# Convolution and FFT-mixer kernel: weights prepared one pass earlier, last bias on ScalarE, products nobody reads in the first slots, and another order of the last slots

## The reference

```python
# layer 0: depthwise convolution, 25x25 taps of which every third is kept and the middle one is 0
lat = conv(x, raw_kernel * mask, padding='SAME', feature_group_count=96)
x = lat * x + bias + x
# layer 1, part 1: tokens t = 3025 positions of each image
h = relu(bn1(ln(t) @ w1.T))                       # 96 -> 192
X = fft(h, axis=tokens, norm='ortho')             # 3025 points
xr = relu(X.real * rd - X.imag * idg + rb)        # rd, idg: diagonals of r and i
xi = relu(X.imag * rd + X.real * idg + ib)
t = t + bn2(ifft(xr + 1j * xi, norm='ortho').real @ w2.T)
# layer 1, part 2: feed-forward net whose operands are rounded to fp8 (5 bit exponent, 2 bit mantissa)
h = relu(qlinear(ln(t), W1, b1))                  # 96 -> 384
t = t + qlinear(h, W2, b2)                        # 384 -> 96
```

## Time and profile before

| | |
|---|---|
| median of three runs | 4942.9 us |
| profiled execution | 4928.84 us |
| its span | 4927.0 us |
| busy: PE, DVE, ACT, POOL | 91%, 74%, 74%, 46% of the span |
| convolution | from the start to about 868 us |
| mixer | from about 868 us to the end |

### The profile page before, as it was taken

How to read it: one execution, slowest core, us unless ns; L and a number is a source line. 1 busy time by engine, 2 the same in 40 slices (tenths; PEclk the granted TensorE clock), 3 DMA queues, 4 the chain that set the end, 5 groups by cost and what they waited for, 6 DMA issues and landing times.

```text
span 4927.0 us, 170278 instructions
## 1 busy us (share of the span) xinstructions
PE 4496.8 (91%) x64799; PEld 3663.0 (74%) x64799; DVE 3649.5 (74%) x10911; ACT 3659.7 (74%) x7819; POOL 2281.3 (46%) x2602
## 2 busy tenths in 40 slices
PE   7999997699999999999999999999999999999964
PEld 6888886477777777777777777777777777777742
DVE  5444446247888888888888888888888888888865
ACT  3444443378888888888888888888888888888843
POOL 2433542144555555555555555555545455555532
PEclk9999998599999999999999999999999999999965
DMA  6877785366666666666666666666666666666541
GB/s 177 249 250 224 238 252 173 105 170 193 179 184 182 186 181 181 184 185 180 183 187 184 189 185 188 181 178 186 184 179 186 176 184 184 182 186 187 164 96 30
DMA packets 787283, 895.64 MB, mean 182 GB/s; under 512 B 241723, under 2 KB 694776, under 8 KB 774392
## 3 DMA queue, kind: packets, MB, share of 16 engines
q1 hardware_dynamic: 786200, 884.64, 63.4%
q10 hardware_dynamic: 288, 0.11, 0.0%
HBM read 500.00 MB, written 384.61 MB: 180 GB/s over the span
## 4 chain that ended last, share of the span: by engine, by line
PE 57%; DVE 12%; ACT 8%; issue 4%; DMA 0%; DVEq 0%; POOL 0%; POOLq 0%; SPq 0%; ACTq 0%
PE ps L1138 13%; PE ps L1125 10%; ACT y L912 7%; PE ps L1157 7%; PE ps L1233 5%; PE ps L1166 4%; PE ps L1182 4%; PE ps L1222 4%; PE ps L1196 4%; PE ps L1209 3%; PE ps L1112 2%; DVE y L995 1%; DVE bn L1048 1%; DVE xn L1033 1%; DVE var L972 1%
## 5 line engine op out<-in xcount | busy, mean ns | idle before, releaser
L789 POOL TENSOR_SCALAR gv<-gv 128x400 f32<-128x400 f32 (+1 forms) x512 | 489.6, 956 | 1663.8 <-DVE xn L1033 1433.7
L1138 PE MATMUL ps<-hid,fa 121*128 121x384 f32 (+1 forms) x2048 | 805.9, 476 | 43.0 <-DVE t L1057 30.8
L554 PE MATMUL cps<-toep,xin 114*128 114x190 f32 (+2 forms) x3456 | 780.7, 340 | 67.5 <-DVE xo L519 32.1
L912 ACT ACTIVATE y<-ps 128x1089 f16<-128x1089 f32 (+1 forms) x512 | 573.2, 1120 | 311.8 <-PE ps L1222 311.8
L395 ACT ACTIVATE xo<-cps 128x180 f32<-128x180 f32 (+3 forms) x576 | 367.3, 638 | 463.2 <-PE cps L557 463.1
L1125 PE MATMUL ps<-w1t,xnt 97*121 97x192 f32 x3200 | 707.0, 332 | 2.9 <-issue 2.1
L519 DVE SCALAR_TENSOR_TENSOR xo<-cps,xo 128x180 f32<-128x180 f32 (+3 forms) x576 | 361.5, 629 | 429.6 <-ACT xo L395 429.0
L554 PEld LDWEIGHTS cps<-toep,xin 114*128 114x128 f32 x3456 | 534.2, 195 | 133.7 <-issue 43.0
L1001 DVE CAST hq<-y 128x1092 fp8e5<-128x1092 f16 (+1 forms) x512 | 537.1, 1049 | 53.4 <-DVE y L995 0.9
L866 ACT ACTIVATE hid<-ps 121x384 f32<-121x384 f32 (+1 forms) x1024 | 438.9, 429 | 169.8 <-PE ps L1125 169.7
L995 DVE TENSOR_SCALAR y<-y,b1q 128x364 f16<-128x364 f16 (+1 forms) x1536 | 477.9, 366 | 105.4 <-ACT y L912 105.4
(11 more groups left out here) (110 smaller groups left out, 9702.3 us busy)
## 6 DMA issues: line engine op xcount, KB each, us to landing
a_d<-arow SPq DMA_DIRECT2D x448, 288.0 KB, 4.5
acol<-a_d SPq DMA_DIRECT2D x384, 300.0 KB
xin<-in_items SPq DMA_DIRECT2D x96, 1008.0 KB
g_d<-mixed SPq DMA_DIRECT2D x512, 150.0 KB
tok<-x_d SPq DMA_DIRECT2D x64, 1134.4 KB
out<-o_sb SPq DMA_DIRECT2D x448, 136.1 KB
x_d<-xo SPq DMA_DIRECT2D x48, 990.0 KB, 12.2
grow<-g_d SPq DMA_DIRECT2D x128, 312.0 KB, 10.5
```

Source lines behind the costliest of these rows:

```text
L554: last = nc.tensor.matmul(ps[2 * (m % DEEP)][:, (r0 - o0) * GC:(r1 - o0) * GC], xb, toep[e % 2][0:GP, c, at * GC:(at + r1 - r0) * GC], sta ...
L789: nc.gpsimd.tensor_scalar(v, v, 0.0, None, ALU.max).then_inc(v_cut, 1)
L912: nc.scalar.activation(y16[n % 2][:, :, 0:w], ps[:, MIXP:MIXP + FM, 0:w], ACT.Copy).then_inc(y16_ready, 1)
L1138: nc.tensor.matmul(ps[0:M, ROW, 0:(s1 - s0) * H], fa[:, :], hid[part][:, 0:s1 - s0, :].rearrange("p j h -> p (j h)"), start=True, stop=Tru ...
```

## The change

It has seven parts.

1. The preparation of the weights moves from pass 1 to the second half of pass 0 (VectorE before items 18, 22, 25, 28, 30, 32 and 34, ScalarE's roots before item 20).
2. The item biases of the last pass move from VectorE to ScalarE.
3. SyncE waits for the tokens of image 0 before it issues the tables `fb` and `ib`.
4. TensorE gets products that nobody reads (`keep_busy`, identity by identity, 128x128, into bank 7): 40 ahead of the slots, 2 and 3 at two places of each slot 0 to 15, and 10 ahead of the first `columns`.
5. Behind the last inverse (slots from `DRAIN` = 528) `down` writes bank 0 and goes last in the slot on TensorE, `out_down` goes last on ScalarE, and `up` no longer waits for `z_ready` of the chunk before.
6. `gate_sum` is cut into three functions and a semaphore `b_ready` is added to its first instruction; VectorE's `larger` waits for it. The order of these instructions stays.
7. `widen_bias` is cut in two and some offsets are written in another way (`RES` as `ROWS + 1` and the like), with no instruction moved.

```diff
+DRAIN = CHUNKS + INV + 1
...
         @block.scalar
         def _(act):
+            def bias_item(t, n):
...
+                act.wait_ge(gated, t * PER + n + 1)
+                v = xo[k][e % 2][:, :, n % DIL::DIL, n // DIL]
+                nc.scalar.activation(v, v, ACT.Identity, bias=cbias[:, c:c + 1]).then_inc(biased[1], 1)
...
-                    if t == 1 and n == 2:
+                    if t == 0 and n == 20:
                         act.wait_ge(w_var, 1)
...
+                    if t == PASSES - 1 and n:
+                        bias_item(t, n - 1)
+            bias_item(PASSES - 1, PER - 1)
...
-                    if t == 1 and n == 0:
+                    if t == 0 and n == 18:
                         shift_variances()
-                    if t == 1 and n == 6:
+                    if t == 0 and n == 22:
                         invert_roots()
-                    if t == 1 and n == 14:
+                    if t == 0 and n == 25:
                         refine_roots()
...
-                    if t == PASSES - 1 and n:
-                        bias_item(t, n - 1)
-            bias_item(PASSES - 1, PER - 1)
...
+        def down_bank(n):
+
+            return DOWNP if n + DOWN < DRAIN else 0
...
                 if g == FIRST + 1:
+                    sp.wait_ge(tok_in[0], 16)
                     sp.dma_start(fb[:, :, :], p["c_fb"]).then_inc(tables_in, 16)
...
+            def gate_imag(t):
...
+                nc.scalar.activation(spectrum(t, 0), column(t, 1), ACT.Abs,
+                                     scale=idg[:, hf:hf + 1]).then_inc(b_ready, 1)
...
+            for g in range(DRAIN, LAST + 1):
+                if here(g - TURN2 - 1):
+                    out_turn2(g - TURN2 - 1)
+                if g % NS == 6 and 0 <= (g + 2) // NS < B + 5:
+                    root((g + 2) // NS)
+                if here(g - UP):
+                    out_up(g - UP)
+                if here(g - DOWN):
+                    out_down(g - DOWN)
...
                 dve.wait_ge(c_ready, t + 1)
+                dve.wait_ge(b_ready, t + 1)
                 nc.vector.tensor_tensor(sv, column(t, 0), sv, ALU.max).then_inc(m_ready, 1)
...
-                pe.wait_ge(y16_ready, n + 1)
+                if n + DOWN < DRAIN:
+                    pe.wait_ge(y16_ready, n + 1)
+                else:
+                    pe.wait_ge(v_ready, CHUNKS)
+                    pe.wait_ge(m_ready, CHUNKS)
...
-                        last = nc.tensor.matmul(ps[:, DOWNP, C * j:C * (j + 1)],
+                        last = nc.tensor.matmul(ps[:, down_bank(n), C * j:C * (j + 1)],
...
-                    pe.wait_ge(z_ready, n)
+                    pe.wait_ge(z_ready, min(n, DRAIN - DOWN))
...
+            def keep_busy(times):
+                for _ in range(times):
+                    nc.tensor.matmul(ps[:, DOWNP, 0:128], ident[:, :], ident[:, :], start=True, stop=True)
+
+            keep_busy(40)
+            for g in range(FIRST, DRAIN):
+                filling = 0 <= g < GATE + 6
+                if g == GATE:
+                    keep_busy(10)
...
+                if filling:
+                    keep_busy(2)
                 if here(g - 1):
                     rows(g - 1, 1)
                 if here(g):
                     widen(g, 0)
                 if here(g - MIX):
                     mix(g - MIX)
+                if filling:
+                    keep_busy(3)
                 if here(g):
                     rows(g, 0)
...
+            for g in range(DRAIN, LAST + 1):
+                if here(g - ROWS):
+                    inverse_rows(g - ROWS)
+                if here(g - UP):
+                    up(g - UP)
+                if here(g - TURN2):
+                    turn2(g - TURN2)
+                if here(g - DOWN):
+                    down(g - DOWN)
```

More of the change, by code:

```diff
@@ L997, in widen_bias, with cast @@
                 last.then_inc(relu_ready, 1)
+            def cast(n):
+                w = (tokens(n)[1] - tokens(n)[0]) * U
+                w += w % 2
+                y, q = y16[n % 2], hq[n % 2]
                 if n >= 2:
@@ L1071, in _ @@
                 k, c = (g + 2) // NS, g % NS
-                if here(g - RES):
-                    residual(g - RES)
+                if here(g - ROWS - 1):
+                    residual(g - ROWS - 1)
                 if c == 6 and 0 <= k < B + 5:
```

69 lines of the change are left out of this document (39 added, 30 removed).

## The result

The changed kernel takes 4830.0 us (median of 4 runs, 4823.6 to 4838.0) against 4945.2 us (median of 4, 4940.8 to 4949.2; a fourth run has moved it from 4942.9) for the kernel before: ratio 0.9768, 95% interval 0.9751 to 0.9786, so 115 us or 2.3% faster. The forecast was 4822, its range 4795 to 4858: inside the range, and 8 us slower than forecast.

A forecast was written before the change was run, and what follows sets the result against it. The prediction took TensorE to bound the long middle, and waits between engines the four stretches around it. Gains of 18.3 + 22.8 + 4.5 + 18 + 5 + 51.7 = 120.3 us from 4942.9 gave 4822 us, range 4795 to 4858.

The forecast's parts named there:

- Slots 10 to 16: Mixer slots after the fill, 40.7 us before, partly at the low clock: gain 5 us (0 to 8).
- Weights in pass 0: Convolution pass 1: parameter instructions no longer blocked by GpSimd's bias once moved to pass 0; gain 18.3 us (15 to 18.5).
- Last bias on ScalarE: Convolution pass 15: item bias no longer waits for GpSimd, ScalarE fits copy and bias; gain 22.8 us (18 to 23).
- a sign of being wrong: Convolution pass 15: the prediction would be wrong if ScalarE's bias took over 0.6 us.
- Tokens ahead of the tables: Start of the mixer: first tokens arrive sooner when loaded without the tables; gain 4.5 us (2 to 6).
- Unread products: Mixer's fill: products close TensorE's holes and raise its clock to 2.4 GHz; gain 18 us (-1 to 26).
- rival 1: Mixer's fill: clock stays at 1.2 GHz, gains of 18 and 5 us fall away, total 4846 us; chance 0.13.
- Drain: Slots 528 to 553: two chunks in the chain at once, 97.6 us instead of 149.3; gain 51.7 us (20 to 64).
- GpSimd against VectorE: Drain: GpSimd's additions now fall beside VectorE's work, only bias and cast meeting them; cost 0.25 us a slot, 6 in all.
- Rival 2: Drain: GpSimd's lock holds VectorE 1.48 us on each of 25 slots, 31 us above charge, total 4853 us; chance 0.12.
- The middle: Long stretch between fill and drain: bound by TensorE at full clock, the change moves nothing there.
- rival 4: Middle: new semaphore and doubled waits stretch each of 510 slots; at 0.3 us the kernel takes 4975 us; chance 0.02.

The follow-up runs named there:

- e1: Kernel before, with only the preparation of the weights moved from pass 1 to pass 0: 4923 us, ratio 0.9961.
- e2: Kernel before, with only the item bias of the last pass moved from VectorE to ScalarE: 4917 us, ratio 0.9946.
- e3: Kernel before, with only the drain's change (`down` last in its own bank, its copy last, `up` without the late `z_ready`): 4898 us, ratio 0.9909.
- e4: Changed kernel with all unread products taken out: 4852 us, ratio 0.9821 to the kernel before.
- e8: Changed kernel with the tables loaded together with the first tokens instead of behind them: 4839 us, ratio 0.9806 to the kernel before.
- e10: Changed kernel without the 40 products ahead of the first turn, the others kept: 4832 us, ratio 0.9782 to the kernel before.
- e7: Changed kernel with its unread products on the 8-bit 121x121 identity, same number: 4855 us, ratio 0.9840 to the kernel before.
- e9: Changed kernel without the five products a slot in slots 0 to 15, the 40 and the 10 kept: 4856 us, ratio 0.9836 to the kernel before.
- e5: Changed kernel with GpSimd's two additions in the drain covering only 2 of 96 columns, output incomplete: 4815 us, ratio 0.9758 to the kernel before.
- e11: Changed kernel with four more unread products behind `down` in every slot of the drain: 4820 us, ratio 0.9760 to the kernel before.

## Why the prediction was right, and which terms were off

The five mechanisms with a kernel of their own stood: weights (e1), bias (e2) and drain (e3) alone, products (e4) and the order of tokens and tables (e8) by taking them away. Slots 10 to 16 have no run of their own. The sum was 120.3 us against 115 measured (interval of the ratio: 106 to 123), and the terms were on the whole too high: measured one by one they add up to some 110. The terms:

*Weights in pass 0*: predicted 18.3. The profiled pair showed 15.5 at the start of pass 2 and 12.9 at that of pass 15, and I first took that for a loss; over all profiles it is 17.1 and 18.5, with single ones up to 7 us apart. Right within that.

*Last bias on ScalarE*: predicted 22.8, measured 22.9 in the pair and 22.0 to the last item in e2. I had priced the bias at 0.50 us and it takes 0.60 to 0.63, which I had named as a sign of being wrong. It did no harm, because the bias starts 0.21 us before the copy has ended (789.83 against 789.52 + 0.52), so that the pair takes 0.91 us (789.52 to 790.43). The Trainium skill (ScalarE: Activation LUTs, What ACT_TABLE_LOAD costs) gives some 93 ns for the operand and as much overlap with a neighbour. The rows agree on the operand, about 0.10 us more than the copy, and not on the overlap, which is about twice that. With one overlap of 93 ns my estimate would have been 1.00; the 0.91 of the prediction takes it off twice, once at each end of the pair, and in the rows only one end overlaps. That it met the measured 0.91 is luck.

*Tokens ahead of the tables*: predicted 4.5, measured 2.8 in the pair and 3.2 by e8. The sum divided bytes by the common rate of tokens and tables; alone the tokens were there 9.65 us after their issue, against 880.43 - 867.98 = 12.45 before, with the tables beside them.

*Unread products*: predicted 18 up to slot 10, measured 19.4, but two errors cancel. A product was priced at 0.21 us at 1.2 GHz from the pitch of three transpositions; it takes 0.22 at 2.4 GHz and twice that at 1.2. The slot became 3.90 and not 3.6 for it. Against that the clock stayed high through the whole stretch, where I had let some of it fall. The 40 ahead were costed as free and are, but they are also worth nothing (e10), and the reason for rival 1's low chance was weaker than written: e7 had the holes halved and TensorE 92% busy, and the clock stayed at 0.50. With its products rival 1 was the outcome, so that the products of the change were enough was in part luck.

*Slots 10 to 16*: predicted 5, measured 0.9 in the pair. The clock is up (0.91 against 0.68), but the pitch is now 6.75 us from `columns` to `columns` in five of six slots, where before it went from 5.05 to 8.16. TensorE waits there 5.5 us for VectorE's gating, against 2.7 before: what the clock gives goes in good part into this wait. This is the term that was furthest off for its size. The pair is also at the low end: in the six kernels without products in these slots the stretch takes 39.6 to 43.0 us (e9, e4), 41.5 in the mean, and in the seven with the 32-bit products 37.5 (e5) to 39.9, 39.4 in the mean, so some 2 us is the better figure. Why kernels with the same work there differ by up to 3 us is open.

*Drain*: predicted 51.7, measured 46.0. The step that was mis-sized is "GpSimd against VectorE", charged with 0.25 us a slot or 6 in all: e5 gives 15.9, of which up to 2 may be its clock. Its reason was too narrow as well: the prediction let only bias and cast meet GpSimd's additions, and the root chains and the norm were held too (4.1 us by e5). The rest of the sum was then 91.6 against 87.4 measured in e5, 4 us too high, so that two errors partly cancel here as well. `down` came 4.63 us apart up to slot 541 and 3.59 behind it, not 3.6 and 2.8. Rival 2, which charged 31 us more for the lock, was right in kind and came true by a third. Where the additions meet VectorE's bias, as at 4733.59, the slot pays 0.95 us; the mean over 25 slots is 0.64.

The Trainium skill (SBUF — State Buffer, Who interferes with whom) describes the lock as exclusive for the whole instruction. The rows agree where VectorE's bias goes from 0.75 to 1.70 us beside 1.57 us of additions. An estimate from the rows: if all of GpSimd's time had held VectorE, it would have cost 25 times 1.48 us, 37 us, and it took 15.9. The rest of GpSimd's time met instructions that were not held (statistics and residual) or idle time.

*The middle*: nothing moved and rival 4 is out, but it was 7.2 us longer in the pair. In the profiles of all fourteen kernels, whose middles do the same work, it took between 3612.0 (e11) and 3633.6 us (e10), and the 3614.4 of before is near the short end. The four kernels without `b_ready` take 3622.9 in the mean and the ten with it 3624.1, so the new semaphore and the doubled waits, which the prediction put at nothing, cost no more than the wander hides. That wander, with the one of the convolution, is why 107 us of stage gains in the pair, 110 by the terms and 115 by the medians agree no closer.

## What to carry to other kernels

When a chain through several engines is opened, add up what each engine works in a slot, and then look which instructions of VectorE and GpSimd will now lie at the same time: here 0.95 of the 4.32 us of a slot went into that meeting, and moving VectorE's bias and cast to ScalarE was worth 22 us more. Products that nobody reads paid here where no hole of TensorE was left in the trace; the same number of shorter ones, or those ahead of the stage with idle time behind them, brought nothing. Look where the clock stands when the real work begins, not only whether the products raised it. And a stage gain is to be compared over several executions before a loss is explained: the 2.6 us that I took as "lost on the way" lie within a wander of up to 7 us.
